# Three-layer CIN tower on one core: early w2, its mixing moved, the first tile's rows written by ScalarE, nine unread matmuls

## What is computed

```
e = stack([tbl_f[ids[:, f]] for f in range(39)], axis=1)      # 512 x 39 x 16
prev = e
for k in range(3):                                            # 128 units each
    z = einsum('bmd,bhd->bdmh', e, prev).reshape(b, D, m * h)
    t = transpose(z @ w[k] + bias[k])                         # b x 128 x 16
    t = t / sqrt(sum(t * t over units and d))
    logit.append(t); prev = t
z = sum over d of concat(logit)                               # 512 x 384
h = relu([z, dense_ctx] @ W_top1 + b_top1)
y = relu(h @ W_top2 + b_top2) @ W_top3
```

## Time and profile before

| | us |
|---|---|
| median of 3 runs | 1170.16 |
| lowest and highest | 1168.98, 1170.77 |
| the profiled execution | 1173.38 |
| its span | 1171.6 |
| TensorE busy | 1120.3 |
| DVE busy | 994.8 |
| POOL busy | 946.5 |
| ACT busy | 144.6 |

### The profile page before, as it was taken

How to read it: one execution, slowest core, us unless ns; L and a number is a source line. 1 busy time by engine, 2 the same in 40 slices (tenths; PEclk the granted TensorE clock), 3 DMA queues, 4 the chain that set the end, 5 groups by cost and what they waited for, 6 DMA issues and landing times. The chain is left out here.

```text
span 1171.6 us, 22368 instructions
## 1 busy us (share of the span) xinstructions
PE 1120.3 (96%) x8252; PEld 612.8 (52%) x8252; DVE 994.8 (85%) x875; ACT 144.6 (12%) x298; POOL 946.5 (81%) x646
## 2 busy tenths in 40 slices
PE   0788999999999999999999999999999999999999
PEld 0344555555555555555555555555555555555553
DVE  2658989899898989989898998988999898999782
ACT  0001111101111110111111011111101011110102
POOL 5566889798888979898897989889798988958680
PEclk9898999999999999999999999999999999999999
DMA  6886637293653718275472827547282844728010
GB/s 181 252 273 222 200 104 265 67 320 92 241 181 127 251 65 328 75 261 161 143 245 68 318 71 270 152 152 247 72 303 71 284 138 168 236 69 300 1 51 1
DMA packets 102345, 205.81 MB, mean 176 GB/s; under 512 B 49915, under 2 KB 52923, under 8 KB 102326
## 3 DMA queue, kind: packets, MB, share of 16 engines
q1 hardware_dynamic: 95312, 203.29, 51.7%
q0 software_dynamic: 5120, 1.29, 1.1%
q10 hardware_dynamic: 1894, 0.96, 0.4%
HBM read 203.05 MB, written 2.46 MB: 175 GB/s over the span
## 5 line engine op out<-in xcount | busy, mean ns | idle before, releaser
L642 DVE TENSOR_TENSOR z<-t_ps,xb 128x2048 f32<-128x2048 f32 (+2 forms) x352 | 711.1, 2043 | 68.0 <-PE acc L822 43.5
L340 POOL TENSOR_TENSOR sums<-z,sums 128x1024 f32<-128x1024 f32 x224 | 531.6, 2373 | 53.8 <-DVE sums L655 38.7
L808 PE MATMUL acc<-z,w_sb 128*64 128x512 f32 x1408 | 327.6, 601 | 16.5 <-DVE z L642 10.7
L822 PE MATMUL mix_ps<-sums,s_sb 128*64 128x256 f32 x1792 | 330.8, 380 | 2.0 <-POOL sums L340 0.8
L337 POOL TENSOR_TENSOR sums<-z 128x512 f32<-128x512 f32 x192 | 245.7, 1280 | 83.6 <-DVE z L642 79.4
L822 PE MATMUL acc<-z,w_sb 128*64 128x256 f32 x896 | 269.4, 383 | 0.2
L822 PE MATMUL mix_ps<-z,w_sb 128*64 128x256 f32 x896 | 269.4, 383 | 0.0
L822 PE MATMUL acc<-z,s_sb 128*64 128x256 f32 x896 | 267.9, 381 | 0.0
L822 PE MATMUL p_ps<-z,w_sb 128*64 128x256 f32 x896 | 267.9, 381 | 0.0
L822 PEld LDWEIGHTS mix_ps<-sums,s_sb 128*64 128x64 f32 x1792 | 187.2, 137 | 99.3 <-POOL sums L340 13.5
L822 PE MATMUL acc<-sums,w_sb 128*64 128x256 f32 x896 | 230.9, 380 | 0.0
(11 more groups left out here) (80 smaller groups left out, 447.7 us busy)
## 6 DMA issues: line engine op xcount, KB each, us to landing
xb<-xt SPq DMA_DIRECT2D x128, 512.0 KB, 6.5
xb<-xq SPq DMA_DIRECT2D x112, 512.0 KB, 5.1
xb<-xt SPq DMA_DIRECT2D x48, 768.0 KB, 6.8
xr<-xt SPq DMA_DIRECT2D x47, 468.0 KB
x<-xt SPq DMA_DIRECT2D x15, 234.0 KB
xr<-xt SPq DMA_DIRECT2D x15, 234.0 KB
gathered<-in_table,rows_of POOLq DMA_INDIRECT x160
xt<-gathered SPq DMA_DIRECT2D x16, 72.0 KB, 2.3
```

What stands on the lines that cost most here:

```text
L340: nc.gpsimd.tensor_tensor(t41, b2, t2_twice, ALU.subtract).then_inc(t41_ready, 1)
L642: nc.vector.tensor_tensor(z[:, at:at + n, :], t_ps[k - 1][:, :].rearrange("p (a n) -> p a n", a=1).broadcast_to([P, n, N]), xb[:, XB_ROW[c ...
L808: last = nc.tensor.matmul(acc[k][o, :], w_sb[k][:, field + r, o], z[:, at + r, :], start=(c == 0 and r == 0), stop=(c == NCH - 1 and r == ...
L822: return nc.tensor.matmul(bank[side, cols], weights, moving, start=start, stop=stop, skip_group_check=True)
```

## The change

1. w1 and w2 are laid out on the host so that a partition's 39 rows lie in one piece (`by_unit`), and both are loaded at the start, w2 right behind w1.
2. Parts 1 and 2 of w2's mixing stand behind the first layer 0 product of tile 0, parts 3 and 4 behind the fourth and the fifth product of layer 1. Tile 1's layer 0 products stand where the other tiles have them: three groups behind the tenth product, one behind the eleventh.
3. `write_rows` is taken out of SP's function; tile 0's rows are written by ACT.
4. In tile 0 SP writes the mixed rows of tile 1 behind the layer 0 loads of tile 1.
5. TensorE waits for the last gather of tile 0 and does five matmuls whose result nobody reads, then layer 0, one more, the norm's matmuls, three more. They write to `mix_ps`, which layer 1 begins anew.

```diff
+WARM = (5, 1, 3)
@@ sync
-            sp.dma_start(w_sb[1][:, :, :], w1.rearrange("(m h) o -> h m o", h=P)).then_inc(w_loaded[1], 16)
+            sp.dma_start(w_sb[1][:, :, :], w1).then_inc(w_loaded[1], 16)
+            sp.dma_start(w_sb[2][:, :, :], w2).then_inc(w_loaded[2], 16)
...
-            write_rows(0)
             write_mixed(0)
...
                 if c == NCH // 2:
 
-                    write_rows(1)
-                    write_mixed(1)
-            sp.dma_start(w_sb[2][:, :, :], w2.rearrange("(m h) o -> h m o", h=P)).then_inc(w_loaded[2], 16)
+                    write_rows(sp, 1)
             sp.wait_ge(xt_written, 96)
             sp.wait_ge(acc0_ready, 1)
             load_layer0(1)
+            write_mixed(1)
@@ scalar
+            write_rows(act, 0)
             act.wait_ge(xt_written, 48)
@@ vector
-                    if c == NCH - 2 and first:
-                        mixed_weights(2, 0)
-                    if c == 9 and not first and not last:
+                    if first and c in (3, 4):
+                        mixed_weights(2, c - 1)
+                    if c == 9 and not last:
                         products0(i + 1, (0, 1, 2,))
-                    if c == 10 and not first and not last:
+                    if c == 10 and not last:
                         products0(i + 1, (3,))
-                if first:
-
-                    products0(i + 1, range(len(LOADS0)))
-                    for part in range(1, 4):
-                        mixed_weights(2, part)
...
-            products0(0, range(len(LOADS0)))
+            products0(0, (0,))
+            for part in range(2):
+                mixed_weights(2, part)
+            products0(0, range(1, len(LOADS0)))
@@ tensor
+            def keep_busy(n):
+
+
+                for _ in range(n):
+                    nc.tensor.matmul(mix_ps[:, :], w0_sb[:, 0, :],
+                                     w0_sb[:, 0:N // UNITS, :].rearrange("p k o -> p (k o)"), start=True, stop=True)
...
             pe.wait_ge(ones_ready, 1)
+            pe.wait_ge(last_gathered, 16)
+            keep_busy(WARM[0])
             layer0(0)
+            keep_busy(WARM[1])
             add_partitions(0, 0, 1)
+            keep_busy(WARM[2])
             tile(0, first=True)
```

More of the change, by code:

```diff
@@ L279, in load_shifted, with write_rows, write @@
             engine.dma_start(xr[:, k0:k1, :].rearrange("p k n -> p (k n)"), src).then_inc(xr_loaded[g], 16)
+        def write_rows(engine, i):
+            def write(first, g0, g1, fields=GROUP):
+                blk = xt[bass.ds(i, 1), first:first + (g1 - g0 - 1) * GROUP + fields, :].rearrange(
+                    "a (g f) (b d) -> (a f b) g d", f=fields, d=EMB)
+                engine.dma_start(blk, gathered[0:fields * TILE_B, g0:g1, :]).then_inc(xt_written, 16)
+            engine.wait_ge(rows_gathered, 16 * (GROUPS - 1) * (i + 1))
+            write(0, 0, GROUPS - 1)
+            write(FIELDS, 0, (XT_ROWS - FIELDS) // GROUP)
+            engine.wait_ge(last_gathered, 16 * (i + 1))
+            write((GROUPS - 1) * GROUP, GROUPS - 1, GROUPS, LAST_GROUP)
         block = ctx.enter_context(nc.Block())
@@ L371, in _ @@
             sp.dma_start(w0_sb[:, :, :], w0a).then_inc(w0a_loaded, 16)
-            sp.dma_start(w_sb[1][:, :, :], w1.rearrange("(m h) o -> h m o", h=P)).then_inc(w_loaded[1], 16)
-            def write_rows(i):
-                def write(first, g0, g1, fields=GROUP):
-                    blk = xt[bass.ds(i, 1), first:first + (g1 - g0 - 1) * GROUP + fields, :].rearrange(
-                        "a (g f) (b d) -> (a f b) g d", f=fields, d=EMB)
-                    sp.dma_start(blk, gathered[0:fields * TILE_B, g0:g1, :]).then_inc(xt_written, 16)
-                sp.wait_ge(rows_gathered, 16 * (GROUPS - 1) * (i + 1))
-                write(0, 0, GROUPS - 1)
-                write(FIELDS, 0, (XT_ROWS - FIELDS) // GROUP)
-                sp.wait_ge(last_gathered, 16 * (i + 1))
-                write((GROUPS - 1) * GROUP, GROUPS - 1, GROUPS, LAST_GROUP)
+            sp.dma_start(w_sb[1][:, :, :], w1).then_inc(w_loaded[1], 16)
+            sp.dma_start(w_sb[2][:, :, :], w2).then_inc(w_loaded[2], 16)
             def write_mixed(i):
@@ L443, in _ @@
                 load_fields(i)
-                write_rows(i + 1)
+                write_rows(sp, i + 1)
                 write_mixed(i + 1)
@@ L957, with by_unit @@
                 w0b[j::PER_STEP, k] = w0[(h + s) % FIELDS, h]
+    def by_unit(w):
+        return np.ascontiguousarray(w.reshape(FIELDS, UNITS, UNITS).transpose(1, 0, 2))
     second = (np.arange(P) % TILE_B >= TILE_B // 2).astype(np.float32)
@@ L965 @@
         "dense_t": np.ascontiguousarray(a["dense_ctx"].T), "w0a": w0a, "w0b": w0b,
-        "w1": a["L0_rec_w1"], "w2": a["L0_rec_w2"], "b0": a["L0_rec_b0"], "b1": a["L0_rec_b1"],
+        "w1": by_unit(a["L0_rec_w1"]), "w2": by_unit(a["L0_rec_w2"]), "b0": a["L0_rec_b0"], "b1": a["L0_rec_b1"],
         "b2": a["L0_rec_b2"], "wt1": a["W_top1"], "bt1": a["b_top1"], "wt2": a["W_top2"], "bt2": a["b_top2"],
```

## The result

The changed kernel takes **1164.99 us** (median of 7 runs, 1162.18 to 1166.27); the kernel before, measured beside it, 1170.16 (7 runs, 1168.98 to 1173.04). The ratio is 0.9944, 95% interval 0.9931 to 0.9956: 6.6 us by the ratio, 5.2 by the medians. Faster, as forecast, but by about half of 12.2, and 2.2 us above the range (1154.0 to 1162.8). The profiled execution has a span of 1164.4 (time 1166.27), before 1171.6. It is the longest of the seven: three of them, with a granted clock of 0.994 over the whole span, took 1165.80 to 1166.27 us, the other four, with 0.997, 1162.18 to 1164.99.

The account below looks back on a forecast made before the run. TensorE, busy 96% of the span, was taken as the bound, with gains where it idles or runs at half clock. Gaps -14.2, layer 1 clock -0.3, layer 0 -1.2, start +3.5: -12.2 from 1170.16, 1158.0 us, range 1154.0 to 1162.8.

Parts of the forecast that it names:

- Part 1: Early w2 with its mixing moved: TensorE's gaps of 5.81 and 4.08 us and half-clock stretches behind them go, 14.2 us won.
- Part 5: SP's queue in tile 0: tile 1's mixed rows written after its layer 0 loads; worth 0 itself, Part 1 rests on it.
- no gap of over 1 us between 68 and 110: Sign for TensorE: layer 2 of tile 0 right behind tile 1's layer 0, near 87 us, at clock 1.00, without such gaps.
- one part is 1.16 us: Cost on DVE of each moved part of w2's mixing, taken as covered by waits, so nothing lost up to the sixth product.
- Part 3: Layer 0 of tile 0: five unread matmuls ahead of it raise TensorE's clock, 1.2 us won, between 0 and 2.4.
- The rival that they don't hold the clock: Unread matmuls leave layer 0 and the start of layer 1 as before: 1159.5 us, up to 1.9 more; chance 0.08.
- Part 4: Start of the program: the early w2 load delays tile 0's gathered rows and all behind, costing 3.5 us, between 0 and 7.7.
- a gather that lands only when the stream has drained: One way to Part 4's cost: gathers seen at 22 us or somewhat later, 3.6 us later or more.
- a gather that is seen 5.2 us behind its issue: Other way to Part 4's cost: tile 0's ninth gather, issue over at 15.82, seen at 21.0, 2.5 us later than before.
- the first rival: The start waits for the whole weight stream at the old 277 GB/s: 7.7 instead of 3.5 us, 1162.2 us; chance 0.15.
- nor by nothing: Rival: gathers and xt writes take turns with w2 at no loss, so 3.5 falls away: 1154.5 us; chance 0.13.
- xr of tile 1 wasn't late: Rival that it is late: the eleventh product waits for tile 1's xr, about 0.5 us slower than before; chance 0.03.

Follow-up runs that it names:

- e1: Changed kernel with parts 3 and 4 of w2's mixing behind tile 0's layer 0 products, ahead of the norms: 1161.68 us, ratio 0.9917.
- e4: e1 plus two pairs of unread DVE additions in layer 1, each pair one with a PSUM input and one with both inputs in SBUF: 1161.86 us.
- e3: Changed kernel with eight instead of five unread matmuls ahead of layer 0 and three more in its gap behind the first group: 1163.27 us, ratio 0.9924.
- e6: Changed kernel with the edits of e1 and e3 together: 1161.53 us, ratio 0.9915.
- e10: e6 with x and xr of tile 1 loaded ahead of the eleventh chunk's xb rows and tile 1's rows written behind the fourth chunk: 1162.53 us, ratio 0.9911.
- e11: e6 with tile 1's rows written from ACT's queue behind the first norm instead of SP's: 1163.53 us, ratio 0.9923.
- e2: Changed kernel without its nine unread matmuls and the wait for the last gather: 1165.1 us, ratio 0.9929.
- e7: Changed kernel with w1 and w2 in their old layout, 39 pieces of 512 bytes a partition: 1169.27 us, ratio 0.9981.
- e5: Changed kernel with SP waiting for the first nine gathers of tile 0 before issuing w2's load: 1168.36 us, ratio 0.9969.
- e12: Changed kernel with e1's edit and without the nine unread matmuls (e2's edit): 1162.79 us, ratio 0.9921.
- e9: Kernel before with the nine unread matmuls alone added: 1171.14 us, ratio 1.0000.

## Why the prediction was right in sign and short in size

On the profiled executions the forecast span was 1159.4 and the measured one 1164.4: 5.0 us. They fall on three steps.

**Part 1, "nothing is lost and nothing won on DVE": wrong, 2.0 us.** The two gaps it took away are away; the eleventh product waits for no xr, and Part 5 (SP's queue) holds. Its sign "no gap of over 1 us between 68 and 110" failed by the wait of 1.21 at 73.95. The step that failed is the cost of the moved mixing, "one part is 1.16 us". That row was from a place where POOL didn't add; between products 4 and 6 POOL's sums run all the time, and part 4 costs 3.90 and holds POOL up as well. Up to the fifth product the forecast holds (8.5 us behind the first, forecast 8.6); the sixth comes 2.5 us too late. Layer 1 took 37.35 us to tile 1's layer 0 against the 35.3 of the forecast. e1 brings it to 34.26, e4 shows the mechanism. The trace of before had what was needed: `w_sb<-w_sb` has both inputs in SBUF, and the first row has 1.26 for such a part.

**Part 3, layer 0's clock: wrong, 2.0 us.** The term was −1.2, its ends 0 and −2.4; in the profiled execution it measured +0.8 (7.57 against 6.76), outside the ends. The doubt was put in the right place ("what gaps of 1 to 3 do it doesn't tell"), but the end was set at the pace of before, as if unread matmuls could only help. (Nor does 1 to 3 follow from its numbers: 4.4 or 9.2 us out of 9.7 leave 0.5 to 5.3. The gap measured 3.12.) Before, layer 0's steps got to full pace on the way (6.76); in the profiled execution of the changed kernel they ran slow throughout (7.57). Kernels with the nine showed 7.57, 7.59, 6.18, 6.21, 6.18 and 4.51, kernels without them 6.76, 6.69, 4.51 and 4.51, one profiled execution each: no advantage. The size of this step is that of the longest of seven executions; what it is in the median one isn't shown. Only with matmuls in the gap as well (e3, e6, e10, e11) was it 4.51 each time. The rival that they don't hold the clock (0.08) was what happened in layer 0; in layer 1 they did hold it (1.94 for the first four matmuls), and it was worth nothing: layer 1 took 37.35 us with them and 37.34 without (e2).

**Part 4, the start: right in its number, in part by luck; 1.0 us missing behind it.** +3.5 forecast, +3.3 measured (21.79 against 18.46). The rate was 411 GB/s, more than the 387 assumed. The Trainium skill's 512 B for line rate (DMA: Bandwidth & Descriptors, Specifications) would have left 277; this case's rows and e7, which goes back to pieces of 512 B and to 281 GB/s, decide against it. Of the two ways to the 3.5, "a gather that lands only when the stream has drained" isn't what happens: in e7 the stream is 7 us longer and the rows are seen at 22.07 all the same. The other, a gather that is seen 5.2 us behind its issue beside long loads, is nearer: the ninth was seen 6.0 us behind it here and 6.3 in e7 (issue over at 15.84 and 15.80). What waits for the end of the stream are the writes, which land near 28 in e5 and 29 in e7, some 2 us behind it. So the first rival (7.7 us) is e7 in its price, not in its path: not 26 but 22.07 for the gathered rows, which are written only at 29.08, and DVE's last layer 0 products start at 40.30, 4.6 us behind the changed kernel's, where the rival had 4.2 more.

What the step left out is the rest of the chain. DVE's last three layer 0 products start at 35.73, 4.5 behind 31.25, **1.0 us** more than Part 4: against the kernel before, the writes of xt took 0.4 us more (3.3 against 3.0) and the reading of x and xr, from SP's issue at 25.11 on, 0.8 (10.6 against 9.8). w2's stream isn't the cause, it was through at 19.5. The same reading took 9.8 and 9.7 us in e2 and e12 and up to 11.4 in other profiled executions; why is open.

**The baseline.** 12.2 was the difference to an execution of 1173.4 us and was taken off a median of 1170.16. The measured difference of the two profiled executions is 7.2, that of the medians 5.2. The executions of one kernel differ by 4 us, and the pace of tile 0's layer 0 (4.51 to 7.59 in these profiles) is the largest thing in them that no edit accounts for; the reading of xr (9.7 to 11.4) is another. Part of what was taken off may not be there in the median execution. That this is the 2.0 isn't shown.

So 12.2 = 7.2 + 2.0 + 2.0 + 1.0; why 7.2 became 5.2 (6.6 by the ratio) is open. The range was missed because two terms at a cost of nothing (the mixing) or a sure gain (the clock) had no end on the other side.

Of the rivals, the start wasn't held by 7.7, nor by nothing; xr of tile 1 wasn't late in the changed kernel (DVE waits for it in the experiments in which the rest is faster: e1, e6, e10 to e12).

## What to carry to other kernels

An instruction has the duration of its row only beside the same neighbours: when moving a DVE operation with two SBUF inputs, look at what POOL does at the new place. A microsecond won early shows at the end only as far as the next arrival that doesn't move with it (e6), so measure each part of a change alone; here the layout of two loads was worth 0.7 of the whole, and nine unread matmuls nothing that could be measured (1.2 us either way, e9). One profiled execution of each kernel isn't enough to price a term that differs between executions. Set a bound on the loss side for every step taken as free.

## What the runs showed of the hardware that wasn't expected

- A DVE addition with two SBUF inputs and an addition of POOL's exclude each other for a whole instruction: 3.90 us instead of 1.16 for two instructions, 1.99 instead of 1.28 on POOL, 1.01 instead of 0.30 for a small one. A gather issued by POOL beside it changes nothing (1.16 at 79.12).
- Writes in pieces of 64 bytes on one queue get little of the DMA engines while another queue streams long ones: 10.8 us for 118 KB beside w2's load, 3.3 us behind it, and over 14 us from the end of their issue (52.1) beside xb's loads (e11). The gathers were held less: rows seen 3.3 to 4.5 us later beside a full stream (21.79 against 18.46 and 17.26), whether it ended at 19.5 or at 27. The Trainium skill (DMA: Bandwidth & Descriptors, Queues, rings and completion order) has the engines take turns between queues by packets; turns by packets are not turns by bytes, and these runs give the price.
- One contiguous row of 19,968 bytes a partition against 39 pieces of 512 bytes: 411 against 277 and 281 GB/s, at full busy shares of the engines in all three. Behind such a load in 4,992 pieces the next issue on the same queue stood 14.73 and 9.62 us; behind one of 128 rows 0.86 and 0.44.
- Five unread matmuls ahead of layer 0 didn't keep it at full pace: its last five steps took 4.51 to 7.59 us in six profiled executions with them and 4.51 to 6.76 in four without. With eight ahead of it and three in its gap they took 4.51 in all four. A granted clock of 1.00 can stand beside matmuls at half pace: in e2_no_warm the stretches 28 to 33 and 33 to 36 show 1.00, and the four matmuls at 31.29 take 3.68 us instead of 1.94.
